# The order of the first layer's work: a rank for every piece in place of a repeating pattern

## The chip, the cores and the metric

The kernel runs on one core of a Trainium2 chip. The metric is the device time of one execution in microseconds (us); lower is better. The engines are PE (TensorE: matrix products; its loads of the fixed operand are shown apart as PEld), ACT (ScalarE), DVE (VectorE), POOL (GpSimd) and SP (SyncE, which here only starts DMAs). Each runs its own list of instructions in order, and they wait for each other on semaphores.

## The reference, cut to what matters

The whole computation has four layers of two branches each. The change touches the first layer alone. Its input is x of 2 x 1024 rows of 128. One branch puts x through eight blocks:

```python
def _block(x, p):                       # eight times, L0_attn
    residual = x
    q = x @ Wq + bq; k = x @ Wk + bk; v = x @ Wv + bv
    Q = elu(q) + 1.0; K = elu(k) + 1.0
    KV = einsum('nsh,nsh->nh', K, v);  Ksum = K.sum(axis=1)
    Z = 1.0 / (Q * Ksum[:, None, :] + EPS_Z)
    V = Q * KV[:, None, :] * Z
    attn = gelu(V @ Wo + bo)
    x = layernorm(attn + residual, ln1_s, ln1_b)
    residual = x
    h = gelu(x @ Wf1 + bf1)             # 512 wide
    ff = gelu(h @ Wf2 + bf2)
    return layernorm(ff + residual, ln2_s, ln2_b)
```

The other is a softmax attention of 16 heads of 8 columns over the same x:

```python
scores = einsum('bhqd,bhkd->bhqk', q, k) / sqrt(8)
attn = softmax(scores, axis=-1)
o = einsum('bhqk,bhkd->bhqd', attn, v)
```

What follows (output projection, a mixture of experts, three further layers) is the same in both kernels.

## The kernel before

`layer_0_branches` does both branches at once. The data are laid with the 128 features on the partitions.

**The eight blocks.** The 2048 rows are cut into four streams `s` of 512 columns. Each stream goes through eight blocks `i`. One block of one stream has 16 products of 128x128 by 128x512 in float32 on PE: `k`, `q`, `v`, `o`, `n1centre`, `n1var`, `f0` to `f3`, `ff` (four in one), `n2centre`, `n2var`. All are issued by the helper `product` (L110). A float32 product shows as two MATMUL records, two passes. Between them ACT does `exp_k`, `relu_k`, `exp_q`, `relu_q` (L586, L588), `log_z`, `z` (L592, L596), the gelus `gelu_o`, `h0` to `h3`, `gelu_ff` (L566) and the logarithm and exponential of the norms (L573, L577). DVE does the sums, products and norm scaling: `Q` and `K` at L671, `mix` at L688, `res1` and `res2` at L692 and L696, `n1copy` and `n2copy` at L653. POOL squares (L734), and at the end adds each stream to x (L738).

**The attention.** It is cut into 16 chunks `m`. A chunk has 16 units of `search` (L498: a pair of bf16 products into a PSUM buffer of 128x1024, whose maximum DVE takes in `maximum`, L708), one `turn` of the maxima (L507), 16 units of `weigh` (L523: the same scores less their maximum, into such a buffer, whose exponential ACT takes in `weight`, L622), 8 pieces of `use` (L540: the weights times the values, four 128x32 float32 products side by side on the array's columns), then `out` (L629), `sums` (L551), `log` (L638), `inverse` (L642) and on POOL a division (L744). SP carries the maxima into `qs` (L427), loads the next block's weights and later sets of `qs` and `ks`.

**The buffers.** `search` and `weigh` share two double PSUM buffers in the order in which PE comes to them: a unit can be issued when the unit two before it has been read, by DVE for a `search` and by ACT for a `weigh` (`double_free`). All other outputs but that of `use` share three single banks in the same way (`single_free`). So the order on PE also says which buffer a unit waits for. ACT needs one table for gelu and another for exp and log, and a table load stands wherever its order goes from one to the other (`logs` and `gelu`).

**What sets the order.** Each engine's work is written as several generators (the four streams, `search`, `weigh`, `use` and so on). A generator yields a planned number and then issues its instructions; `in_order` always lets the generator with the lowest number go on. The numbers are only compared, nothing waits for a time. Before, they come from a pattern of length `PERIOD = 44.0`: block `i` of stream `s` stands at `(2 * i + s // 2) * PERIOD` plus an entry of `PLAN_ATT` or `PLAN_NET`, chunk `m` at `m * PERIOD` plus an entry of `PLAN_CHUNK`. So the order of one period repeats, called a round below, and each round holds two blocks of streams and parts of three chunks.

Of the kernel before, what the change touches and what calls it, by code (L numbers as in the profile page):

```python
# [227 lines left out]
class Ring:  # L228
# [25 lines left out]
BUFS = 3  # L254

PERIOD = 44.0
PLAN_ATT = {
    "q": (3.88, 0.80), "k": (-0.00, -3.02), "v": (5.37, 1.59), "exp_k": (0.98, -1.86), "relu_k": (1.52, -0.11),
    "exp_q": (6.24, 2.05), "relu_q": (6.77, 4.58), "less_k": (3.19, -1.17), "K": (4.35, 0.58), "less_q": (13.24, 11.61),
# [4 lines left out]
PLAN_NET = {  # L264
# [5 lines left out]
PLAN_CHUNK = {  # L270
    "search": (10.34, 14.80, 15.01, 18.78, 18.99, 22.65, 22.86, 29.45, 31.73, 36.64, 37.86, 39.71, 42.80, 48.77, 51.26, 54.14),
    "maximum": (12.12, 15.22, 17.08, 19.20, 20.26, 23.42, 24.48, 29.86, 32.17, 37.06, 38.27, 40.77, 43.22, 49.19, 51.67, 54.55),
    "negate": (55.92,), "turn": (59.40,), "turn_copy": (60.83,),
# [8 lines left out]
def layer_0_branches(core, w_att, w_f1, w_f2, wa, col, att_landed, cols_landed, q_dram, k_dram, qs, ks, stacks, values, later, mixed):  # L282
# [29 lines left out]
    def att(s, i, name):  # L312
        return (2 * i + s // 2) * PERIOD + PLAN_ATT[name][s % 2]

    def net(s, i, name):
        return (2 * i + s // 2 + 1) * PERIOD + PLAN_NET[name][s % 2]

    def chunk(m, name, i=0):
        return m * PERIOD + PLAN_CHUNK[name][i]

# [3400 lines left out]
```

## Time and profile before

| what | value |
|---|---|
| median of three runs | 1711.33 us |
| the three runs | 1709.41, 1711.33, 1718.65 us |
| the profiled execution | 1713.21 us, its span 1711.5 us |
| PE busy over the span | 1571.5 us (92%) |
| first layer's branches in the trace | about 30.4 to 822 us |
| mean granted TensorE clock | 0.964 of full |

The profile was taken of one more execution, whose own time is 1713.21 us; 1.7 us of it lie outside of the span from the first to the last instruction. The rows are from that execution. In a timeline a row is one group of like instructions that follow each other: its start, its length to the end of the last, the engine and line, what is written and read, how many, and in brackets the idle time of the engine before it with what ended it. The ends of matmuls are modelled, so the distance from one start to the next is the surer reading.

### The profile page before, as it was taken

Reading aid. Unit: us, or ns where it says so; the run is one execution under the profiler, and the core shown is the slowest. Engines: PE = TensorE matmul, PEld = TensorE weight load, DVE = VectorE, ACT = ScalarE, POOL = GpSimd, SP = SyncE. Lnnn points to the kernel's source line nnn. Section 1 sums busy time; section 2 is a strip of 40 time slices with the busy share of each in tenths; the row PEclk is TensorE's granted clock in tenths of the full one; section 3 lists DMA queues with packets and bytes.
Section 4 is the critical chain, followed back from the end, with each engine's and each line's share of the span. In section 5 each row is a group of like instructions: output and inputs, shape, how many; then the busy total and the mean of one; then the engine's idle time right before and its main releaser. Section 6 shows DMA issues by size and latency. Waiting matters only on the chain. (4 is left out here: it accounts for less than half of the span.)

```text
span 1711.5 us, 19967 instructions
## 1 busy us (share of the span) xinstructions
PE 1571.5 (92%) x7054; PEld 682.4 (40%) x7054; DVE 1224.6 (72%) x1736; ACT 1151.8 (67%) x1604; POOL 262.1 (15%) x227
## 2 busy tenths in 40 slices
PE   6999999999999999999799989999877678678998
PEld 3333233333333333332344446665432455333674
DVE  5977777777777777773143325876399889997997
ACT  5688888888888888888333357534475568333663
POOL 1000111111010111111000010000179200582000
PEclk8999999999999999999999988999999889888999
DMA  6200101010010100000252112111353677630000
GB/s 199 57 12 7 25 13 26 13 25 13 7 25 7 25 13 7 13 0 1 60 101 62 37 39 64 46 39 44 99 191 130 204 232 249 177 132 12 1 1 25
DMA packets 66716, 104.18 MB, mean 61 GB/s; under 512 B 9015, under 2 KB 32534, under 8 KB 66596
## 3 DMA queue, kind: packets, MB, share of 16 engines
q1 hardware_dynamic: 55354, 65.15, 14.0%
q10 hardware_dynamic: 9216, 33.56, 6.0%
q0 software_dynamic: 2048, 4.20, 0.8%
q8 instruction: 57, 0.93, 0.2%
q14 instruction: 41, 0.34, 0.1%
HBM read 86.92 MB, written 15.87 MB: 60 GB/s over the span
## 5 line engine op out<-in xcount | busy, mean ns | idle before, releaser
L708 DVE TENSOR_REDUCE best<-quad 128x2 f32<-128x1024 f32 x256 | 309.7, 1221 | 130.5 <-PE quad L498 128.1
L622 ACT ACTIVATE weights<-quad 128x1024 f32<-128x1024 f32 x256 | 255.8, 1029 | 28.6 <-PE quad L523 28.2
L2629 PE MATMUL quad<-l_st,ident 128*128 128x512 f32 x256 | 130.3, 653 | 44.3 <-DVE l_st L2940 44.2
L540 PE MATMUL quad<-weights,values 128*32 128x512 f32 x1024 | 136.4, 605 | 0.4 <-ACT weights L622 0.4
L110 PE MATMUL quad<-q,wf 128*128 128x512 f32 x256 | 121.5, 606 | 0.7 <-DVE q L659 0.3
L110 PE MATMUL quad<-hid,wf 128*128 128x512 f32 x256 | 116.6, 599 | 0.0
L566 ACT ACTIVATE hid<-quad,col 128x512 f32<-128x512 f32 x128 | 84.9, 689 | 21.4 <-PE quad L110 21.2
L734 POOL TENSOR_TENSOR sq_all<-cen_all 128x512 f32<-128x512 f32 x64 | 65.2, 1039 | 213.9 <-DVE cen_all L653 213.9
L110 PE MATMUL quad<-sq_all,mean_w 128*128 128x512 f32 x176 | 94.7, 638 | 1.8 <-ACT sq_all L1367 0.9
L498 PE MATMUL quad<-ks,qs 48*128 48x512 bf16 x512 | 89.5, 385 | 6.8 <-DVE best L708 6.3
L2629 PEld LDWEIGHTS quad<-l_st,ident 128*128 128x128 f32 x256 | 50.7, 209 | 112.3 <-DVE l_st L2940 60.3
L523 PE MATMUL quad<-qs,ks 49*128 49x512 bf16 x512 | 91.5, 384 | 2.2 <-ACT weights L622 2.2
L744 POOL TENSOR_TENSOR mixed<-mixed,inv 128x512 f32<-128x512 f32 x16 | 20.3, 1269 | 465.9 <-ACT inv L642 465.9
L2528 POOL DMA_INDIRECT slots<-l_rows,l_blocks_index x32 | 82.0, 2562 | 42.0 <-ACT l_rows L2746 32.5
L110 PE MATMUL quad<-cur,wa 128*128 128x512 f32 x168 | 87.0, 627 | 0.0
L2923 DVE TENSOR_TENSOR l_st<-l_u,l_bs 128x1024 f32<-128x1024 f32 x64 | 76.5, 1221 | 10.7 <-PE quad L2629 10.7
L523 PEld LDWEIGHTS quad<-qs,ks 49*128 49x128 bf16 x512 | 22.2, 93 | 146.8 <-issue 60.4
L1391 ACT ACTIVATE end_hid<-quad,end_w1s 128x512 f32<-128x512 f32 x64 | 42.9, 688 | 53.5 <-PE quad L110 51.7
L2940 DVE TENSOR_TENSOR l_st<-l_st,l_c_rows 128x1024 f32<-128x1024 f32 x64 | 75.5, 1213 | 0.1
L2931 DVE TENSOR_TENSOR_SCAN l_st<-sq_all,l_st 128x1024 f32<-128x1024 f32 x32 | 71.9, 2276 | 2.2 <-ACT sq_all L2863 2.2
L110 PEld LDWEIGHTS quad<-q,wf 128*128 128x128 f32 x256 | 45.7, 189 | 66.4 <-issue 64.7
L2931 DVE TENSOR_TENSOR_SCAN l_st<-cen_all,l_st 128x1024 f32<-128x1024 f32 x32 | 71.7, 2274 | 0.0
(454 smaller groups left out, 3035.6 us busy)
## 6 DMA issues: line engine op xcount, KB each, us to landing
l_bs<-xd_dram ACTq DMA_DIRECT2D x32, 512.0 KB
l_c_rows<-xd_dram ACTq DMA_DIRECT2D x32, 512.0 KB
end_cs<-comb SPq DMA_DIRECT2D x32, 256.0 KB, 3.9
l_cs<-comb SPq DMA_DIRECT2D x32, 256.0 KB, 3.7
l_weights<-in_F_w SPq DMA_DIRECT2D x30, 257.0 KB, 4.7
wf<-in_L_f SPq DMA_DIRECT2D x16, 256.0 KB, 2.6
l_rows<-in_F_w SPq DMA_DIRECT2D x15, 257.0 KB, 6.0
qs<-q_dram SPq DMA_DIRECT2D x16, 192.0 KB, 3.5
```

The costliest lines, as they stand in the source:

```text
L110: last = nc.tensor.matmul(out[:, c:c + BANK], lhsT, rhs[:, c:c + BANK], start=(n == 0), stop=(n == len(pairs) - 1))
L498: last = nc.tensor.matmul(to[:, par * BANK:(par + 1) * BANK], qs[n % BUFS][rows, slot, qt * P:(qt + 1) * P], ks[n % BUFS][rows, slot, c * ...
L523: last = nc.tensor.matmul(to[:, par * BANK:(par + 1) * BANK], ks[n % BUFS][rows, slot, kt * P:(kt + 1) * P], qs[n % BUFS][rows, slot, c * ...
L540: last = nc.tensor.matmul(out[32 * j:32 * j + 32, :], values[:, kt, GH * g + j, :], weights[p % BUFS][:, j % 2, j // 2, :], start=(kt == 0 ...
L566: return nc.scalar.activation(*args, ACT.Gelu_apprx_tanh, **kwargs)
L622: nc.scalar.activation(weights[p % BUFS][:, slot, :, :].rearrange("p a t -> p (a t)"), doubles.of("weigh", m, i), ACT.Exp, scale=scale).th ...
L708: nc.vector.tensor_reduce(heads[:, :, slot, qt, c], doubles.of("search", m, i).rearrange("p (a t) -> p a t", a=2), AX.X, ALU.max).then_inc ...
L2528: nc.gpsimd.indirect_dma_start(slots_dram, bass.IndirectOffsetOnAxis(blocks.index[:, i, t:t + 1], 0), rows[:, t, :], None).then_inc(scatte ...
L2629: last = nc.tensor.matmul(y[d][:, c:c + BANK], core.ident[:, :], st[n % RING][:, c:c + BANK], start=False, stop=(s == NS - 1), skip_group_ ...
L2923: nc.vector.tensor_tensor(st[n % RING][:, :], u[h][d][:, :], bs[k % 2][:, :], ALU.mult).then_inc(dbx_ready, 1)
L2931: nc.vector.tensor_tensor_scan(out=st[i][:, :], data0=da[i], data1=st[i][:, :], initial=0.0, op0=ALU.mult, op1=ALU.add).then_inc(scanned, 1)
L2940: nc.vector.tensor_tensor(st[n % RING][:, :], st[n % RING][:, :], cs_rows[k % 2][:, :], ALU.mult).then_inc(times_c, 1)
```

## The change

The pattern is replaced by one table, `PLAN_0`, with a rank for each single piece of work: `PLAN_0["q"]` has 32 numbers, one for each stream and block, `PLAN_0["search"]` has 256, and so on. The ranks count up on each engine from 1 (PE to 1088, ACT to 816). The functions `att`, `net` and `chunk` now look the rank up. The DMAs of SP and the divisions and additions of POOL, whose numbers were those of another piece plus a constant, have entries of their own (`load_att`, `load_maxima`, `divide`, ...). `in_order`, the rings of buffers, the waits and all instructions stay as they are; what differs is the order on each engine, hence which buffer a unit gets, and where ACT's table loads fall.

```diff
-PERIOD = 44.0
-PLAN_ATT = {
-    "q": (3.88, 0.80), "k": (-0.00, -3.02), "v": (5.37, 1.59), "exp_k": (0.98, -1.86), "relu_k": (1.52, -0.11),
...
+PLAN_0 = {
+    "q": (5, 95, 231, 367, 500, 639, 772, 907, 3, 90, 229, 358, 496, 628, 770, 905, 14, 159, 294, 436, 572, 703, 838, 979, 28, 158, 295, 427, 561,
+        698, 833, 975,),
...
+    "load_att": (3, 8, 14, 21, 26, 32, 38,),
...
+    def at(name, i):
+        return PLAN_0[name][i]
+
     def att(s, i, name):
-        return (2 * i + s // 2) * PERIOD + PLAN_ATT[name][s % 2]
-
-    def net(s, i, name):
-        return (2 * i + s // 2 + 1) * PERIOD + PLAN_NET[name][s % 2]
+        return at(name, s * B + i)
+
+    net = att
 
     def chunk(m, name, i=0):
-        return m * PERIOD + PLAN_CHUNK[name][i]
+        return at(name, m * (len(PLAN_0[name]) // CHUNKS) + i)
...
-                        yield att(fourth, i - 1, "o") + 1
+                        yield at("load_att", i - 1)
...
-                        yield chunk(m, "inverse") + 1
+                        yield at("divide", m)
```

The line numbers of what follows the table move by 131: L110 stays, L498 becomes L629, L523 becomes L654, L540 becomes L671, L708 becomes L839, L622 becomes L753.

The order on PE at the start of the layer, before. Rows with `xn,wa` are `k`, `q` and `v`, `mq,wa` is `o`, `k,centre_w` a centring, `sq_all,mean_w` a variance, `ks,qs` a `search` (two matmuls a unit):

```order
L110 MATMUL quad<-xn,wa 128x512 x6
L498 MATMUL quad<-ks,qs 128x512 x14
L110 MATMUL quad<-mq,wa 128x512 x2
L110 MATMUL quad<-k,centre_w 128x512
L498 MATMUL quad<-ks,qs 128x512 x2
L110 MATMUL quad<-k,centre_w 128x512
L498 MATMUL quad<-ks,qs 128x512 x2
L110 MATMUL quad<-sq_all,mean_w 128x512
```

The same place with the change:

```order
L110 MATMUL quad<-xn,wa 128x512 x6
L629 MATMUL quad<-ks,qs 128x512 x6
L110 MATMUL quad<-mq,wa 128x512
L629 MATMUL quad<-ks,qs 128x512 x2
L110 MATMUL quad<-mq,wa 128x512
L110 MATMUL quad<-xn,wa 128x512 x2
L629 MATMUL quad<-ks,qs 128x512 x4
L110 MATMUL quad<-k,centre_w 128x512 x2
```

Seven searches stood ahead of the first `o`; now three do, and `k` and `q` of the third stream follow the two `o`.

The order on PE in the middle of the layer, before, the same in each round. `qs,ks` is a `weigh` (two matmuls a unit), `weights,values` a `use` (four):

```order
L523 MATMUL quad<-qs,ks 128x512 x2
L498 MATMUL quad<-ks,qs 128x512 x2
L540 MATMUL quad<-weights,values 32x512 x4
L523 MATMUL quad<-qs,ks 128x512 x2
L540 MATMUL quad<-weights,values 32x512 x4
L523 MATMUL quad<-qs,ks 128x512 x4
L110 MATMUL quad<-sq_all,mean_w 128x512 x2
L523 MATMUL quad<-qs,ks 128x512 x2
L498 MATMUL quad<-ks,qs 128x512 x2
L540 MATMUL quad<-weights,values 32x512 x4
```

The same work with the change, in the fifth round:

```order
L654 MATMUL quad<-qs,ks 128x512 x2
L629 MATMUL quad<-ks,qs 128x512 x2
L110 MATMUL quad<-sq_all,mean_w 128x512
L654 MATMUL quad<-qs,ks 128x512 x4
L671 MATMUL quad<-weights,values 32x512 x8
L654 MATMUL quad<-qs,ks 128x512 x4
L110 MATMUL quad<-sq_all,mean_w 128x512 x2
L629 MATMUL quad<-ks,qs 128x512 x4
L671 MATMUL quad<-weights,values 32x512 x8
```

Two pieces of `use` now mostly stand together (x8), and after a `search` there often comes a single product and then the next pair of score units, where a `use` stood between.

The order on ACT at the end of the layer, before. `hid` are the `h0` to `h3`, `mk` the two `gelu_ff`, `weights` the `weight` units of the last chunk:

```order
L566 ACT_TABLE_LOAD
L566 ACTIVATE hid<-quad,col 128x512 x8
L561 ACT_TABLE_LOAD
L642 ACTIVATE inv<-inv 128x512
L566 ACT_TABLE_LOAD
L566 ACTIVATE mk<-quad,col 128x512 x2
L561 ACT_TABLE_LOAD
L622 ACTIVATE weights<-quad 128x1024 x3
L629 ACTIVATE mixed<-quad 128x512
```

With the change:

```order
L697 ACT_TABLE_LOAD
L697 ACTIVATE hid<-quad,col 128x512 x8
L692 ACT_TABLE_LOAD
L773 ACTIVATE inv<-inv 128x512
L753 ACTIVATE weights<-quad 128x1024 x2
L697 ACT_TABLE_LOAD
L697 ACTIVATE mk<-quad,col 128x512 x2
L692 ACT_TABLE_LOAD
L753 ACTIVATE weights<-quad 128x1024
L760 ACTIVATE mixed<-quad 128x512
```

Two of the last chunk's sixteen `weight` units are moved ahead of the two `gelu_ff`.

## Rows read from the trace of the kernel before

**Rows 1.** The page, busy time, share of the span and instructions of PE.

```profile
PE 1571.5 (92%) x7054; PEld 682.4 (40%) x7054; DVE 1224.6 (72%) x1736; ACT 1151.8 (67%) x1604; POOL 262.1 (15%) x227
```

**Rows 2.** Three stretches: length, busy time by engine (count), clock, DMA share, GB/s.

```profile
30.40:85.00 54.60, 47.15 (x121) 15.93 (x121) 46.13 (x71) 35.26 (x48) 3.48 (x5) 0.87 0.40 112
85.00:776.00 691.00, 690.07 (x2823) 213.88 (x2822) 513.48 (x746) 606.39 (x791) 81.30 (x79) 1.00 0.06 14
776.00:822.00 46.00, 39.35 (x183) 11.54 (x179) 11.12 (x17) 37.24 (x46) 8.57 (x8) 1.00 0.00 1
```

**Rows 3.** The waits of PE from 129 to 786 us: total, times, longest.

```profile
PE quad L523 <- ACT weights L622: 0.4, 1, 0.4
```

**Rows 4.** The timeline of PE in the middle of the layer.

```profile
476.47 0.39 PE L523 MATMUL quad<-qs,ks 49*128 49x512 bf16 x2
476.79 1.07 PE L540 MATMUL quad<-weights,values 128*32 128x512 f32 x8
477.79 0.61 PE L523 MATMUL quad<-qs,ks 49*128 49x512 bf16 x4
478.32 1.98 PE L110 MATMUL quad<-sq_all,mean_w 128*128 128x512 f32 x4
...
480.47 0.38 PE L498 MATMUL quad<-ks,qs 48*128 48x512 bf16 x2
...
482.17 0.39 PE L523 MATMUL quad<-qs,ks 49*128 49x512 bf16 x2
482.49 1.12 PE L110 MATMUL quad<-sq_all,mean_w 128*128 128x512 f32 x2
483.55 0.39 PE L523 MATMUL quad<-qs,ks 49*128 49x512 bf16 x2
...
500.39 4.56 PE L110 MATMUL quad<-q,wf 128*128 128x512 f32 x10
504.88 0.60 PE L498 MATMUL quad<-ks,qs 48*128 48x512 bf16 x4
```

**Rows 5.** The page, costliest groups: busy, mean ns of one, idle before.

```profile
L708 DVE TENSOR_REDUCE best<-quad 128x2 f32<-128x1024 f32 x256 | 309.7, 1221 | 130.5 <-PE quad L498 128.1
...
L110 PEld LDWEIGHTS quad<-q,wf 128*128 128x128 f32 x256 | 45.7, 189 | 66.4 <-issue 64.7
```

**Rows 6.** The timeline of PE at the start of the layer.

```profile
43.74 0.61 PE L498 MATMUL quad<-ks,qs 48*128 48x512 bf16 x2 [1.12 <-DVE best L708]
45.47 0.61 PE L498 MATMUL quad<-ks,qs 48*128 48x512 bf16 x2 [1.12 <-DVE best L708]
...
47.25 3.78 PE L110 MATMUL quad<-mq,wa 128*128 128x512 f32 x4
```

**Rows 7.** The timeline of DVE at the start of the layer.

```profile
43.59 0.68 DVE L671 SCALAR_TENSOR_TENSOR q<-q,mq 128x512 f32<-128x512 f32 x1
44.19 2.35 DVE L708 TENSOR_REDUCE best<-quad 128x2 f32<-128x1024 f32 x2
46.46 1.40 DVE L688 SCALAR_TENSOR_TENSOR mq<-q,totals,mk 128x512 f32<-128x512 f32 x2
```

**Rows 8.** A stretch at the start: length, PE busy (count), clock, DMA share, GB/s.

```profile
46.00:50.00 4.00, 3.43 (x8) 0.50 0.54 115
```

**Rows 9.** The timeline of ACT at the end of the layer.

```profile
795.33 0.69 ACT L566 ACTIVATE mk<-quad,col 128x512 f32<-128x512 f32 x1 [2.48 <-PE quad L110]
796.03 1.28 ACT L561 ACT_TABLE_LOAD   x1
797.33 2.86 ACT L622 ACTIVATE weights<-quad 128x1024 f32<-128x1024 f32 x3
...
816.69 0.60 ACT L629 ACTIVATE mixed<-quad 128x512 f32<-128x512 f32 x1 [0.68 <-PE quad L540]
```

**Rows 10.** The timeline of POOL at the end of the layer.

```profile
810.86 1.27 POOL L738 TENSOR_TENSOR x<-x,cur 128x512 f32<-128x512 f32 x1 [4.61 <-DVE cur L659]
...
819.84 1.26 POOL L744 TENSOR_TENSOR mixed<-mixed,inv 128x512 f32<-128x512 f32 x1 [2.48 <-ACT inv L642]
```

More of the change, by code:

```diff
@@ L392, in block_weights @@
                         sp.dma_start(wa[:, :], w_att[i]).then_inc(att_landed, 16)
-                        yield net(fourth, i - 1, "f3") + 1
+                        yield at("load_f1", i - 1)
                         sp.wait_ge(st.pe_done[third], spe.value("f3", i - 1))
@@ L396, in block_weights @@
                         sp.dma_start(wf1[:, :], w_f1[i]).then_inc(f1_landed, 16)
-                        yield net(fourth, i - 1, "ff") + 4
+                        yield at("load_f2", i - 1)
                         sp.wait_ge(st.pe_done[third], spe.value("ff", i - 1))
@@ L415, in sets @@
                     for n in range(BUFS, len(SETS)):
-                        yield chunk(2 * (n - BUFS) + 1, "use", PAIRS - 1) + 2
+                        yield at("load_set", n - BUFS)
                         sp.wait_ge(weights_used, 2 * PAIRS * (n - BUFS + 1))
@@ L422, in maxima_rows @@
                         n, c = m // 2, m % 2
-                        yield chunk(m, "turn_copy") + 0.5
+                        yield at("load_maxima", m)
                         sp.wait_ge(turned_copied, m + 1)
@@ L734, in stream @@
                             nc.gpsimd.tensor_tensor(st.sq[s], st.cen[s], st.cen[s], ALU.mult).then_inc(st.pool_done[s], 1)
-                    yield net(s, B - 1, "n2affine") + 1
+                    yield at("add", s)
                     pool.wait_ge(st.dve_done[s], sdve.value("n2affine", B - 1))
@@ L747, in second_values @@
                     for g in range(GROUPS):
-                        yield chunk(2 * g + 1, "use", PAIRS - 1) + 3
+                        yield at("second", g)
                         pool.wait_ge(weights_used, 2 * PAIRS * (g + 1))
```

118 lines of the change are left out of this document (108 added, 10 removed), and 48 rows, old and new, of tables (PLAN_0, PLAN_ATT, PLAN_NET).

## The prediction, made before the changed kernel ran

> **What bounds the kernel now.** I read first the busy shares: PE 92% [rows 1]. That is an average over four layers, and the change touches one, so next come the three stretches of that layer [rows 2]. From 85 to 776 us PE is busy 690.07 of 691.00 us at full clock, ACT 606 and DVE 513: PE is the bound, with no other engine near. Ahead of it lie 54.60 us with 47.15 of PE work at a clock of 0.87, behind it 46.00 us with 39.35. Last the waits: from 129 to 786 us PE waited once, 0.4 us [rows 3]. So in the middle an order can gain only by making PE's own work cheaper, and can lose by any wait that it brings; gains by better filling are to be had at the two ends alone, where PE idles 7.5 and 6.7 us.
>
> **PE's own work.** The same matmuls run, but what one costs depends on its neighbours, start to start [rows 4]. A run of five products takes 504.88 - 500.39 = 4.49 us, two 478.32 to 480.24 or 1.92 us, one alone among score units 483.55 - 482.49 = 1.06: about 0.86 each and 0.10 at either end of a run. A `weigh` ahead of a `use` takes 476.79 - 476.47 = 0.32, two units ahead of products 478.32 - 477.79 = 0.53, so a further unit is 0.22. A lone `use` takes 477.79 - 476.79 = 1.00. I laid these distances on the order of all 1088 pieces. Before that gives 765 us. With the change the products and score units come to the same within 0.5 us (products 0.7 less, searches 1.5 less, weighs 1.7 more): runs are cut and joined about equally often. The `use` pieces change: before, one pair among 128 stood together, now 48 follow another `use`. The trace has no such pair that was not held up by a wait, so I bound it. Below: the second costs as a product within a run, 0.86, and the first leaves off its end too, which saves about 0.2 a pair or 10 us. Above: nothing is saved, and some pieces gain a costlier neighbour, +0.6. I take the value of a switch of kind saved once, 0.10: each such pair costs 0.91 + 1.00 in place of about 2.0. 48 x 0.10 = 4.8, with the 0.5 of the rest **-5.1 us**, ends -10 and +0.6.
>
> What decides this is whether the fixed operand of the next `use` is loaded while the last one still streams. A 128x128 load takes 189 ns [rows 5], and in a run a pass starts each 0.45 us (ten in 4.49 [rows 4]), hardly longer than its 512 columns need; so loads are hidden behind passes that use the same rows of the array. The Trainium skill, page "TensorE: Matmul & The Clock Gate", section "The mechanism", says that a weight load overlaps running matmuls "only when row_grp differs"; two `use` pieces both use all rows, so by it the pair saves nothing. The row speaks against that rule, and with the rule this term would be +0.6 rather than -5.1.
>
> **Waits that the new order brings.** A `search` gives its buffer back after DVE's reduction. At the start, where DVE is the limit and PE idles before each, the searches stand 45.47 - 43.74 = 1.73 us apart [rows 6]; that is PE's 0.43, the 1.22 us reduction [rows 5] and the signals. In the old middle the shortest way from a `search` to the unit that takes its buffer is 482.17 - 480.47 = 1.70 [rows 4], a `use` between; no wait is seen there. The new order has 41 places where a `search`, one product and two score units, or the like, leave only 0.31 + 1.06 + 0.22 = 1.59. Each must wait 0.13 to 0.14: 41 x 0.13 = **+5.3 us**. Where the reduction is itself queued behind another DVE operation (0.60 us from 43.59 to 44.19 [rows 7]) or a `weight` behind another on ACT (0.92 each, 2.86 for three [rows 9]), I find about a dozen places short by 0.1 to 0.6, the worst in the fourteenth round where a copy precedes the maximum: **+3.5**. What waits is PE, and all else is behind it.
>
> Chains over two engines are also tighter. After `o` the matching centring needs PE's 1.1, a gelu of 0.69 [rows 9], an addition of 0.68 like that in [rows 7] and signals, 2.7 us; the old order left 1.6 us more than that, the new one in three of 32 places nothing. In four rounds the logarithm of the mixing is put between `h1` and `h3`, with two more table loads in three of them (66 table changes become 72), so `ff` waits for `h3` behind it. Each load is 1.3 us of ACT (796.03 to 797.33 [rows 9]); six are 8 us, and ACT has 691 - 606 = 85 us idle in the middle [rows 2], so they count only where `ff` follows at once. I set these chains at **+2.5**, between 0 and 8 (half a microsecond in each of 16 rounds). The Trainium skill, page "ScalarE: Activation LUTs", section "What ACT_TABLE_LOAD costs", puts a change of table at about 2.66 us with a drain of 1380 ns; here the next activation starts 1.30 us after the load, so the trace does not show that drain. By the page the six would be 16 us of ACT, still under its idle time.
>
> SP's order also moves. What counts there is the maxima: their four DMAs must land before the chunk's first `weigh`. By the same prices the new order leaves 5.7 us or more from `turn` to `weigh` where the old one left 11; no load is queued ahead that waits longer. I put this at 0.
>
> **The start.** Before, seven searches stand ahead of the first `o` on PE, and the reductions keep DVE from `mix`, which runs at 46.46 [rows 7]; the two `o` start at 47.25 [rows 6], and at a clock of 0.50 [rows 8] take 3.8 us. With the change both `Q` come first on DVE, then one reduction, then `mix` of the first stream. Five reductions stood ahead of it, now one; at (46.46 - 44.19) / 2 = 1.13 each `mix` moves to 46.46 - 4 x 1.13 = 41.9, so the first `o` can start near 42.9, the second near 45, and `k` and `q` of the third stream fill PE's time that was idle. Fewer searches are done by then (six in place of seven at 49.5). Going on along both engines by the same distances I come to the first `turn` about 3 us earlier; the reductions that bound this part are as many. I take **-3.5 us**, between -1 and -5. The clock also rises earlier if PE is busy earlier; that is inside this range.
>
> **The end.** ACT idles 2.48 us ahead of the last `gelu_ff` [rows 9]. Two `weight` units now go there, 2 x 0.92 = 1.8 us off a tail in which ACT then works through to 816.69 - 0.68 = 816.0. Against it the last exponential of a norm is put behind `out` (816.69 before), so that POOL's last addition, which ended at 812 [rows 10], ends some 0.6 us later than the last division could have begun. **-1.2 us**, between -2 and +0.5.
>
> **The sum:** -5.1 + 5.3 + 3.5 + 2.5 - 3.5 - 1.2 = +1.5 us. Against the profiled execution, 1713.21, that is 1714.7; its time stands 1.9 above the median of the three runs, so for a median I predict **1713 us**, no change that can be told. About 0.5% (8.6 us) is what a measurement of this kernel can tell from none: faster is below 1702.8, slower above 1719.9.
>
> **Rivals.** (1) *PE's work gets clearly cheaper and the waits are smaller.* Pairs of `use` save their full 0.2 (-10), the short places mostly lie behind time lost elsewhere (+2 in place of 5.3 + 3.5), and the chains hold (+2.5): -10 + 2 + 2.5 - 4.5 - 1.5 = -11.5, 1700 us. For it: the long run of products shows joined pieces at their cheapest. Against it: the distances 1.59 and 1.73 are both read off directly. (2) *DVE's queue, slower.* In each of the 41 short places the reduction must find DVE free. If in four of ten a 0.60 us operation [rows 7] stands ahead of it, a place costs 0.13 + 0.24 = 0.37 and the term is 15 in place of 5.3: +1.5 + 10 = +11.5, 1723 us. It ends on the slower side from a mean of 0.3 a place on. For it: DVE is 513 of 691 us busy in the middle. Against it: I counted most of such cases already and found few; the old order kept 1.70 at least everywhere. (3) *Pairs of `use` save nothing,* which is what the rule on weight loads above would give: -5.1 becomes +0.6, the sum +7.2, 1718.5, still no change that can be told. (4) *The new ranks do not change the order that matters*, that is, all terms are under 1 us: 1711. The order as built speaks against it.
>
> **How the numbers follow.** Forecast 0.42 and rival 4 0.03, both within 0.5%; rival 3 0.13, of which I give 0.04 to a little over the bound; rival 1 0.22; rival 2 0.20. So faster 0.22, same 0.54, slower 0.24. The range runs from 1700 (rival 1) to 1723 (rival 2); cases beyond, all waits and no saving or the reverse, are left with about 2 in 10. The forecast alone, with the ends of its terms, is 1704 to 1720.
>
> **What would show it.** In the changed profile: (a) the pairs of `use` as rows with x16 whose distance to the next row is 1.91 (right) or 2.0 (rival 3) or 1.8 (rival 1); (b) waits of PE in the middle on DVE's reduction, some 40, total 5 us, where there were none; a total over 12 is rival 2; (c) PE's row for the first `o` at about 43 us; (d) the first `turn` about 3 us earlier; (e) ACT without the 2.5 us gap ahead of the last `gelu_ff`, and the layer's last division within 2 us of 819.84 in place of clearly ahead of it. The forecast is wrong if the middle stretch is over 8 us longer or shorter than before, or if anything after the layer differs by more than 2 us.

## The result: seven to nine microseconds slower, and where they are

| | before | changed |
|---|---|---|
| median of ten runs | 1716.91 us (1709.41 to 1721.36) | 1723.76 us (1716.57 to 1729.09) |
| ratio, 95% interval | | 1.005 (1.003 to 1.007) |
| profiled execution, its span | 1713.21 us, 1711.5 us | 1725.14 us, 1723.4 us |
| first product of the layer to its last `sums` | 786.86 us | 794.68 us |

The kernel is slower, by 0.3 to 0.7%, at the border of what can be told. The predicted 1713 us missed by 10.8 us. 5.6 us of that is the base: the three runs given had a median of 1711.33, ten runs of the same kernel 1716.91. The rest is the layer, forecast at +1.5 us and measured at +7.8 in the profiles. Of the twelve executions of the second kernel with new ranks further down, one fell in a slower state (2576.11 us at a granted clock of 0.554) and is left out of its median.

The page of the changed kernel, and three stretches of it with the windows of [rows 2]:

```profile
PE 1582.0 (92%) x7054; PEld 691.1 (40%) x7054; DVE 1237.4 (72%) x1736; ACT 1157.7 (67%) x1610; POOL 268.9 (16%) x227
```

```profile
30.40:85.00 54.60, 48.72 (x124) 16.15 (x123) 47.12 (x72) 35.35 (x49) 2.76 (x5) 0.85 0.43 112
85.00:776.00 691.00, 680.67 (x2769) 217.02 (x2768) 516.28 (x735) 604.11 (x784) 83.34 (x76) 1.00 0.06 14
776.00:822.00 46.00, 45.49 (x219) 13.60 (x217) 18.66 (x25) 41.98 (x52) 8.15 (x7) 1.00 0.01 1
```

In the middle PE is now busy 680.67 of 691 us where it was 690.07, and has issued 2769 passes where it had issued 2823. It is behind; besides, three products (six passes) that stood in the middle before now stand outside of it. These are the landmarks on PE (the first product, the first `weigh`, the last `turn`, the last `sums`), first before, then changed:

```profile
30.48 1.19 PE L110 MATMUL quad<-xn,wa 128*128 128x512 f32 x1 [5.61 <-PEq L811]
...
85.07 0.60 PE L523 MATMUL quad<-qs,ks 49*128 49x512 bf16 x4
...
788.01 0.27 PE L507 MATMUL quad<-ident,neg 128*16 128x128 f32 x1
...
817.34 1.13 PE L551 MATMUL quad<-mixed,spread 128*128 128x512 f32 x2 [0.72 <-ACT mixed L629]
```

```profile
29.72 2.04 PE L110 MATMUL quad<-xn,wa 128*128 128x512 f32 x2 [5.67 <-PEq L942]
...
83.64 0.39 PE L654 MATMUL quad<-qs,ks 49*128 49x512 bf16 x2
...
793.79 0.27 PE L638 MATMUL quad<-ident,neg 128*16 128x128 f32 x1
...
824.40 1.12 PE L682 MATMUL quad<-mixed,spread 128*128 128x512 f32 x2 [0.72 <-ACT mixed L760]
```

Start: 54.59 us before, 53.92 now. Middle, from first `weigh` to last `turn`: 702.94, now 710.15. End: 29.33, now 30.61. What follows the layer takes 894.2 us of one span and 899.0 of the other; over all profiles of this study, whose programs differ in this layer alone, it lies between 891 and 904.3, so that difference says nothing, and the prediction's bound of 2 us on it could not tell anything. Inside the layer like distances repeat to some 10 ns; the changed kernel's middle and that of the run on the start further down, which differs from it in the first chunk alone, are 710.15 and 710.27 us. No kernel was profiled twice, but by this I read differences of tenths of a microsecond there from one profile.

**Work and wait, parted.** The view of PE's waits does not show what happened: from 85 to 793 us it adds up to 9 us, because a wait that is shorter than the modelled end of the matmul ahead of it isn't seen as idle time. The distances from start to start show all of it. I took the price of each kind of piece between each pair of neighbours from the places where neither it nor the next was released within the last 0.2 us, summed these prices over the order (own work), and called the rest of each distance wait, put down to the release it follows:

| middle (us) | length | own work | wait | after a reduction | after an exponential | chains and others |
|---|---|---|---|---|---|---|
| before | 702.94 | 695.1 | 7.8 | 2.2 (16) | 4.8 (60) | 0.4 |
| changed | 710.15 | 683.5 | 26.7 | 11.3 (56) | 6.3 (44) | 8.2 |

(In brackets the number of places; rests under 0.02 us a place are in the wait alone.) Own work is 11.6 us less, waits are 18.9 us more. Not all of the 11.6 is saved: the change puts four more products behind the last `turn` and one less ahead of the first `weigh`, so the middle has three fewer, at 0.86 us each some 2.6 us. Over the whole layer own work falls by 9.5, from 760.4 to 750.9.

A joined pair of `use`, and four of the places after a reduction, both on PE of the changed kernel:

```profile
399.34 1.93 PE L671 MATMUL quad<-weights,values 128*32 128x512 f32 x16
401.20 0.39 PE L654 MATMUL quad<-qs,ks 49*128 49x512 bf16 x2
...
778.45 0.39 PE L629 MATMUL quad<-ks,qs 48*128 48x512 bf16 x2
778.77 1.07 PE L671 MATMUL quad<-weights,values 128*32 128x512 f32 x8
779.77 0.39 PE L654 MATMUL quad<-qs,ks 49*128 49x512 bf16 x2
780.18 0.39 PE L629 MATMUL quad<-ks,qs 48*128 48x512 bf16 x2
...
781.56 0.39 PE L654 MATMUL quad<-qs,ks 49*128 49x512 bf16 x2
781.90 0.39 PE L629 MATMUL quad<-ks,qs 48*128 48x512 bf16 x2
...
783.28 0.39 PE L654 MATMUL quad<-qs,ks 49*128 49x512 bf16 x2
783.61 0.39 PE L629 MATMUL quad<-ks,qs 48*128 48x512 bf16 x2
```

The pair takes 1.86 us, not 2.00. The searches at 778.45, 780.18, 781.90 and 783.61 stand 1.73, 1.72 and 1.71 apart; one `weigh` lies between, so each takes the buffer of the last. From `weigh` to `search` it is 0.41, 0.34 and 0.33 where 0.23 would do. No row has an idle time in brackets, yet PE loses about 0.1 to 0.2 at each. DVE shows the same rhythm from the other side, a reduction each 1.71 us with 0.49 of idle time, waiting for the search that waits for it:

```profile
780.62 1.23 DVE L839 TENSOR_REDUCE best<-quad 128x2 f32<-128x1024 f32 x1 [0.49 <-PE quad L629]
782.33 1.23 DVE L839 TENSOR_REDUCE best<-quad 128x2 f32<-128x1024 f32 x1 [0.49 <-PE quad L629]
784.04 1.23 DVE L839 TENSOR_REDUCE best<-quad 128x2 f32<-128x1024 f32 x1 [0.49 <-PE quad L629]
```

**Something not foreseen: DVE and POOL hold each other up.** Five of PE's six longest waits in the middle (1.47, 1.40, 1.05, 0.77 and 0.74 us) follow DVE operations that took two to four times their time. DVE, POOL and PE of the changed kernel:

```profile
401.71 1.50 DVE L799 TENSOR_SCALAR mq<-mq 128x512 f32<-128x512 f32 x1
403.14 2.34 DVE L839 TENSOR_REDUCE best<-quad 128x2 f32<-128x1024 f32 x2
...
405.69 0.42 DVE L799 TENSOR_SCALAR mq<-mq 128x512 f32<-128x512 f32 x1
```

```profile
401.64 1.30 POOL L875 TENSOR_TENSOR mixed<-mixed,inv 128x512 f32<-128x512 f32 x1 [16.32 <-ACT inv L773]
```

```profile
402.80 0.39 PE L629 MATMUL quad<-ks,qs 48*128 48x512 bf16 x2
404.50 0.39 PE L629 MATMUL quad<-ks,qs 48*128 48x512 bf16 x2 [1.31 <-DVE best L839]
```

L799 takes 0.42 us alone and 1.50 when it begins beside the division: it ends 0.27 us after the division does (403.21 against 402.94). Of the layer's DVE operations that read and write SBUF alone (L787, L790, L799, L819, L823), 15 began while POOL was at work; 12 were stretched, and the other three came in its last 0.25 us. Of 42 that read PSUM (reductions, copies) none was. The other way round, 16 of 18 POOL operations that began beside a DVE operation on SBUF alone took longer than usual, a square up to 1.49 us in place of 1.04. The kernel before had 13 such meetings, always `mix` (L688, 1.07 in place of 0.74) under the division, with slack behind it. This agrees with the Trainium skill, page "SBUF — State Buffer", section "SBUF: two separate sides", by which the two engines share a pair of ports under an exclusive lock.

### The profile page after: what moved, and what is told of

Same layout as the page of the kernel before. It is cut to its first block and busy times, and to the rows that moved or that the text cites. A ratio compares the mean times of both kernels' runs of the same rounds, so it can differ in the third digit from the quotient of the medians.

```text
span 1723.4 us, 19973 instructions
## 1 busy us (share of the span) xinstructions
PE 1582.0 (92%) x7054; PEld 691.1 (40%) x7054; DVE 1237.4 (72%) x1736; ACT 1157.7 (67%) x1610; POOL 268.9 (16%) x227
## 5 line engine op out<-in xcount | busy, mean ns | idle before, releaser
L839 DVE TENSOR_REDUCE best<-quad 128x2 f32<-128x1024 f32 x256 | 308.9, 1222 | 105.8 <-PE quad L629 104.4
L753 ACT ACTIVATE weights<-quad 128x1024 f32<-128x1024 f32 x256 | 255.0, 1028 | 33.0 <-PE quad L654 30.1
L865 POOL TENSOR_TENSOR sq_all<-cen_all 128x512 f32<-128x512 f32 x64 | 70.4, 1117 | 517.1 <-DVE cen_all L784 517.1
L671 PE MATMUL quad<-weights,values 128*32 128x512 f32 x1024 | 127.1, 600 | 0.1
L110 PE MATMUL quad<-q,wf 128*128 128x512 f32 x256 | 123.0, 613 | 0.1
L110 PE MATMUL quad<-hid,wf 128*128 128x512 f32 x256 | 117.5, 601 | 0.9 <-issue 0.5
L629 PE MATMUL quad<-ks,qs 48*128 48x512 bf16 x512 | 90.6, 387 | 9.6 <-DVE best L839 8.5
L110 PE MATMUL quad<-sq_all,mean_w 128*128 128x512 f32 x176 | 95.2, 639 | 1.8 <-ACT sq_all L1498 0.9
L654 PE MATMUL quad<-qs,ks 49*128 49x512 bf16 x512 | 91.3, 384 | 2.4 <-ACT weights L753 0.9
L110 PE MATMUL quad<-cur,wa 128*128 128x512 f32 x168 | 84.4, 617 | 1.7 <-issue 1.5
L654 PEld LDWEIGHTS quad<-qs,ks 49*128 49x128 bf16 x512 | 21.7, 93 | 130.8 <-ACT weights L753 68.2
L110 PEld LDWEIGHTS quad<-hid,wf 128*128 128x128 f32 x256 | 46.3, 190 | 57.7 <-issue 57.7
L110 PEld LDWEIGHTS quad<-q,wf 128*128 128x128 f32 x256 | 44.4, 190 | 57.4 <-issue 42.7
```

Of the source, the lines that this page charges most:

```text
L110: last = nc.tensor.matmul(out[:, c:c + BANK], lhsT, rhs[:, c:c + BANK], start=(n == 0), stop=(n == len(pairs) - 1))
L629: last = nc.tensor.matmul(to[:, par * BANK:(par + 1) * BANK], qs[n % BUFS][rows, slot, qt * P:(qt + 1) * P], ks[n % BUFS][rows, slot, c * ...
L654: last = nc.tensor.matmul(to[:, par * BANK:(par + 1) * BANK], ks[n % BUFS][rows, slot, kt * P:(kt + 1) * P], qs[n % BUFS][rows, slot, c * ...
L671: last = nc.tensor.matmul(out[32 * j:32 * j + 32, :], values[:, kt, GH * g + j, :], weights[p % BUFS][:, j % 2, j // 2, :], start=(kt == 0 ...
L753: nc.scalar.activation(weights[p % BUFS][:, slot, :, :].rearrange("p a t -> p (a t)"), doubles.of("weigh", m, i), ACT.Exp, scale=scale).th ...
L839: nc.vector.tensor_reduce(heads[:, :, slot, qt, c], doubles.of("search", m, i).rearrange("p (a t) -> p a t", a=2), AX.X, ALU.max).then_inc ...
```

## The experiments

All but two are read from one profile each. "Wait" is counted as above.

**POOL's work cut (three runs).** The squares are cut from the second block on, in the first run those of `n1`, in the second those of `n2`; both cut the divisions too, and the third run cuts the divisions alone (the `.then_inc(...)` behind each call is left out here):

```diff
-nc.gpsimd.tensor_tensor(st.sq[s], st.cen[s], st.cen[s], ALU.mult)
+w = 64 if pre == "n1" and i > 0 else TS
+nc.gpsimd.tensor_tensor(st.sq[s][:, 0:w], st.cen[s][:, 0:w], st.cen[s][:, 0:w], ALU.mult)
-nc.gpsimd.tensor_tensor(heads_of(m), heads_of(m), inv[:, :], ALU.mult)
+nc.gpsimd.tensor_tensor(heads_of(m)[:, 0:64], heads_of(m)[:, 0:64], inv[:, 0:64], ALU.mult)
```

> The changed kernel with POOL's work cut: from the second block on the squares of the first norm, and all sixteen divisions, are done for 64 of their 512 columns (the rest is left out); the squares of the second norm and the order of everything stay. In the changed kernel the way from the first weigh (83.64 us) to the last turn (793.79 us) is 710.15 us, against 702.94 before. Theory C: POOL's long operations stretch DVE operations that run beside them (L799 at 401.71 took 1.50 us beside a division, L787 at 682.10 took 1.53 beside a square, each about twice its usual time), and PE's longest waits are behind those. Then here the stretched operations under divisions and first squares are gone (401.71, 444.39, 529.5, 682.10), PE's waits of 1.47 us at 402.8, 0.74 at 444.4 and 1.05 at 682.9 are down to under 0.3, and the way is 4 to 8 us shorter. Theory R: the waits come from the reduction's and exponential's turnaround in the tighter order alone. Then the way is shorter by under 2 us, and those three waits are still there.

Measured: middle 706.75 us, 3.4 shorter. The wait at 444.4 is gone, that at 682.9 is 0.30 in place of 1.05, that at 402.8 is 0.52 in place of 1.47, where under 0.3 was expected.

> As the run with the first norm's squares cut, but here the squares of the second norm (from the second block on) and all divisions are cut to 64 of 512 columns, the rest left out, and the first norm's are whole. Theory C: the two stretches of 1.55 us of L823 at 280.0 and 671.56, which begin under second or first squares that stand in a row of two or three, are gone or smaller in one of the two runs; each wait of PE behind them (0.77 at 280.5, 1.40 at 672.7) goes with it. The way from the first weigh to the last turn is 4 to 8 us shorter than 710.15. Theory R: under 2 us shorter.

Measured: 706.65, 3.5 shorter; the wait of 0.77 at 280.5 is gone, that of 1.40 is 0.61.

> The changed kernel with POOL's sixteen divisions alone cut to 64 of 512 columns (the rest is left out); all squares are whole. With the two runs that cut divisions and one kind of square (middles of 706.75 and 706.65 us against 710.15) this parts POOL's share. The stretched DVE operations under divisions are those at 401.71 (1.50 us) and 444.39 (1.60 us), behind which PE waited 1.47 and 0.74; so the middle should be 2 to 3 us shorter than 710.15, 707 to 708, and the whole of POOL's share is then the sum of the two runs less this one, 4 to 5 us. If the squares matter alone it is within 0.5 us of 710.15.

Measured: 708.18, 2.0 shorter. The same places with the small division, on DVE and POOL:

```profile
401.39 0.55 DVE L799 TENSOR_SCALAR mq<-mq 128x512 f32<-128x512 f32 x1
401.87 2.34 DVE L839 TENSOR_REDUCE best<-quad 128x2 f32<-128x1024 f32 x2
```

```profile
401.31 0.35 POOL L875 TENSOR_TENSOR mixed<-mixed,inv 128x64 f32<-128x64 f32 x1 [16.32 <-ACT inv L773]
```

L799 is back at 0.55. A shorter square also ends its own chain earlier, which could have been the gain instead. But PE's order is the same in these runs, so the distances can be compared piece by piece: in each run nearly all that is gained is gained at three to six places (of 404.50, 446.09, 684.91, 281.61, 674.30, 532.02 and 484.61), all behind stretched operations. If the parts add up, POOL's whole share is (710.15 - 706.75) + (710.15 - 706.65) - (710.15 - 708.18) = 4.9 us of the 18.9. Theory C holds in kind; the first two runs came in under its 4 to 8, and it explains a quarter of the new waits, not most.

**Half of each reduction.** In both kernels:

```diff
-doubles.of("search", m, i).rearrange("p (a t) -> p a t", a=2),
+doubles.of("search", m, i).rearrange("p (a t) -> p a t", a=2)[:, :, 0:256],
```

> The changed kernel, each maximum over 256 of each 512 columns (the other half is left out), so that a reduction takes about 0.65 us in place of 1.22 and DVE is some 145 us less busy. All else is as it was. Every theory in which PE waits for DVE (the turnaround of 1.70 us from a search to the unit that takes its buffer, DVE's queue, and the stretched operations) says that the middle loses most of its 24.6 us of waits, by my count down to under 9, and is 12 to 18 us shorter than 710.15. If the waits were ACT's (table loads, the exponential's turnaround of 1.53), it would be shorter by under 5.

Measured: 700.12, 10.0 shorter, a little under the range. Waits after a reduction fall from 11.3 to 0.9; those after an exponential stay (7.6), and so do the chains (6.4).

> The kernel before, each maximum over 256 of each 512 columns (the other half is left out). Its middle, from the first weigh at 85.07 to the last turn at 788.01, has 5.7 us of waits by my count and was PE-bound; so it stays within 4 us of 702.94, and only the start, where DVE is the limit, is shorter. This is the ground for the term of PE's own work: with the waits on DVE gone from both, the changed kernel's middle should be shorter than this one's by that term. The prediction had 5.1 us; by the distances in the changed kernel's trace (a pair of use in 1.86 us in place of 2.0) I count 11.7. If it is under 3, joined pieces of use save nothing.

Measured: 702.82, as expected. But the changed kernel without these waits is only 2.7 us shorter. That is under the 3 us at which I was to conclude that joined pieces save nothing. The conclusion does not hold, since 16.6 us of other waits were left in the changed kernel, far more than my first count; so this pair could not give own work; the pair with all cover off, below, asks again.

**DVE's and POOL's order alone.** Only the order on these two engines differs, as in

```diff
-    "divide": (14, 18, 23, 32, 34, 40, 45, 54, 58, 65, 66, 71, 76, 83, 87, 89,),
+    "divide": (14, 17, 24, 27, 32, 42, 47, 52, 53, 61, 68, 74, 77, 83, 86, 88,),
```

> The changed kernel with only the ranks of DVE and POOL changed from 80 us on (510 of 768 pieces on DVE, most by one to three places); PE and ACT keep the changed kernel's order word for word, so PE's own work must be the same. The ranks were looked for with the durations and distances of the traces so far, such that a maximum finds DVE free and few DVE operations begin beside one of POOL's. Theory Q (the waits come from what stands ahead on DVE's queue, POOL's stretching counted in): the middle, 710.15 us in the changed kernel, becomes 700 to 703, that is 7 to 10 us shorter; no wait of over 1 us is left. Theory T (PE's own tight order makes the waits, a search with less than 1.70 us to the unit that takes its buffer): DVE's order can't help, the middle stays within 2 us of 710.

Measured: 702.65, 7.5 shorter, with PE's order untouched: theory Q. Chains lost 4.2 us of wait, reductions 2.5. Two fifths of what the middle lost to waits can be had back by when DVE and POOL do things; the 8.8 us that stay after reductions lie at PE's own short distances.

**PE's order alone, from the kernel before.** The old pattern was written as ranks, then those of PE changed.

> The kernel before with only PE's ranks changed from 80 us on (423 of 1088 pieces, most by one to three places); ACT, DVE and POOL keep the old order. 24 pieces of use follow another use where one did, and 200 runs of products stand where 209 did. By the distances in the traces of both kernels (use after use 0.86 to 0.88 us for the first, 0.97 for the last, 1.00 alone) PE's own work in the middle falls from 697.2 us by 4.2, and its waits stay at 5 to 6. Expected middle 697 to 699 in place of 702.94. If a pair of use saves nothing, by the other distances the fall is under 1 us and the middle is 702 to 703.

Measured: 701.34, 1.6 shorter, outside of the range. By the common prices own work is 690.2, 4.9 less with 22 pairs in the middle; but waits rose from 7.8 to 11.1, about 1.5 us of it behind reductions and 2.2 in products and pieces of `use` that came late by other ways. It is the whole case in small: by the count the joined pieces save what they should, and the tighter order gives two thirds of it back.

**Tables.** Both kernels, every gelu of the layer replaced:

```diff
-table[0] = "gelu"
-return nc.scalar.activation(*args, ACT.Gelu_apprx_tanh, **kwargs)
+logs()
+return nc.scalar.activation(*args, ACT.Relu, **kwargs)
```

> The changed kernel with Relu in place of every gelu of the layer, so that ACT needs no second table and its 72 table loads of 1.28 us are gone (the result is another one). PE's own work is the same. By the distances of the traces the chains over ACT (h3 to ff, mix to o, the exponential behind a table load) lose about 4 us of waits in the middle: 706 in place of 710.15. If table loads cause most of the new waits the middle falls below 702; if none, it stays at 709 to 710.

Measured: 705.42, 4.7 shorter.

> The kernel before with Relu in place of every gelu of the layer (the result is another one), so its 66 table loads are gone. Its chains had slack, so the middle should stay at 702.0 to 702.9 in place of 702.94. What the run of the changed kernel without tables gains over this one is what the new order pays for tables.

Measured: 700.76, 2.2 shorter, more than expected: the kernel before paid for tables too. The new order pays 2.5 us more. An activation takes as long with either function (0.69 us), so the loads are what differs.

**The start.** Each search of the first chunk but the first is issued three times:

```diff
+for again in range(3 if m == 0 and i else 1):
     last = nc.tensor.matmul(to[:, par * BANK:(par + 1) * BANK], qs[n % BUFS][rows, slot, qt * P:(qt + 1) * P],
...
```

> The changed kernel with each search of the first chunk but the first one issued three times into the same buffer, with the same result: 0.46 us more work of PE for each, in the time in which PE waits for DVE's reductions (0.9 us ahead of each). It keeps PE busy while DVE is the limit. Theory K (the gain forecast for the start was lost to the clock: 0.50 at 42 to 46 us and 0.81 or less after 54 us, behind idle stretches of PE): the granted clock no longer falls after 50 us and falls less at 42 to 50, and the first turn comes 1 to 3 us earlier than 42.9 us behind the first product. Theory D (DVE is the limit whatever PE's clock is): the first turn stays within 0.5 us of 42.9.

Measured: the clock no longer falls after 54 us, but the first `turn` comes 44.6 us after the first product, 1.7 later. The stretch from 58 to 62 us (length, PE, PEld, DVE, ACT, POOL busy, clock, DMA share, GB/s), in the changed kernel and in this one:

```profile
58.00:62.00 4.00, 4.00 (x9) 0.74 (x8) 2.92 (x5) 2.03 (x4) 0.00 (x0) 0.50 0.00 0
```

```profile
58.00:62.00 4.00, 4.00 (x16) 1.23 (x16) 3.50 (x4) 2.52 (x4) 0.96 (x1) 1.00 0.00 0
```

Neither theory's number came out. The edit also delays each reduction by the extra passes, so it can't part the two; what the clock costs the start is left open.

**All cover off.** Reductions and exponentials halved, no tables, PE untouched, in both kernels. Beside the two edits above:

```diff
+w = 2 * BANK if p < BUFS else BANK
-nc.scalar.activation(weights[p % BUFS][:, slot, :, :].rearrange("p a t -> p (a t)"), doubles.of("weigh", m, i),
+nc.scalar.activation(weights[p % BUFS][:, slot, :, :].rearrange("p a t -> p (a t)")[:, 0:w], doubles.of("weigh", m, i)[:, 0:w],
```

> The changed kernel with light work on the other engines: maxima over 256 of each 512 columns, exponentials of the weights over 512 of 1024 columns after the first three pairs (the rest is left out, stale values stay), Relu for gelu so that no table is loaded. PE's instructions and their order are untouched. If PE's own work is 683.5 us in the middle, as I count it from distances without a wait, and few waits are left, the middle is 684 to 688 in place of 710.15. If own work is really about 690 (5 us less than before), it is over 690.

> The kernel before with the same light work: half maxima, half exponentials, no table loads; PE untouched. By the distances its own work in the middle is 695.1 us, so the middle is 695 to 697 in place of 702.94. The changed kernel's should then be 8 to 11.6 us shorter than this; 5 or less would say that the forecast's 5.1 was right.

First `weigh` and last `turn` on PE, of the changed kernel so lightened and of the one before:

```profile
80.43 0.60 PE L654 MATMUL quad<-qs,ks 49*128 49x512 bf16 x4
...
768.84 0.27 PE L638 MATMUL quad<-ident,neg 128*16 128x128 f32 x1
```

```profile
80.86 0.60 PE L523 MATMUL quad<-qs,ks 49*128 49x512 bf16 x4
...
776.41 0.27 PE L507 MATMUL quad<-ident,neg 128*16 128x128 f32 x1
```

688.41 and 695.55 us. The second is the own work counted for before (695.1) within 0.5. The first is 7.1 us shorter, where 8 to 11.6 was expected, with 4.9 us of waits still found in it, which gives 683.5 again. The three products that the middle of the changed kernel lacks are in the 7.1. From the first `turn` to the last `sums`, where the changed kernel does the same work and two searches more, the lightened kernels take 728.80 and 733.94 us. So 5.1 us of cheaper work are shown by the two spans alone, as much as was forecast; what lies above that, up to some 9.5 over the layer, rests on the count of the waits that are left.

**A version that keeps the saving.** If cheaper work was real and the waits a matter of order, ranks chosen for both should beat both kernels. They were looked for piece by piece with the distances and durations of these traces. The table itself tells a reader nothing; at the place of [rows 4] PE of the second such kernel runs:

```profile
479.32 0.39 PE L546 MATMUL quad<-ks,qs 48*128 48x512 bf16 x2
479.54 0.38 PE L571 MATMUL quad<-qs,ks 49*128 49x512 bf16 x2
479.85 1.92 PE L588 MATMUL quad<-weights,values 128*32 128x512 f32 x16
481.71 0.39 PE L546 MATMUL quad<-ks,qs 48*128 48x512 bf16 x2
481.94 0.38 PE L571 MATMUL quad<-qs,ks 49*128 49x512 bf16 x2
```

A joined pair stands between units that share a buffer, so they are 2.4 us apart and no wait arises.

> The changed kernel with new ranks on PE, ACT, DVE and POOL from 65 us on, looked for with the distances and durations of the traces so far: pairs of use stay joined (40 of them), but a buffer is not asked for before its reader can be done, and DVE operations keep clear of POOL's. If the explanation holds (joined pieces save about 10 us of PE's own work in the middle, and the new waits, not anything in the rest of the program, gave them back), the middle is 689 to 693 us in place of 710.15 and 702.94, and the whole is 9 to 13 us shorter than the kernel before, a ratio of 0.993 to 0.995. If the layer's length is given back in the later layers, the ratio is 1.00.

Measured: middle 698.18 us (own work 685.2, waits 13.0). Whole: median 1708.07 us of six runs, ratio to the kernel before 0.9952 (0.9923 to 0.9981).

> The same made from the order of the kernel before: its start is kept up to 62 us, the ranks after that are new on PE, ACT, DVE and POOL (32 pairs of use joined, 66 changes of ACT's table as before). The middle is 690 to 694 us in place of 702.94, the end about 2 us shorter, the whole 10 to 14 us shorter than the kernel before, a ratio of 0.992 to 0.995. If the gain of joined pairs were not real, the middle could be no shorter than 700.

Measured: middle 697.03 (own work 686.2, waits 10.8). Whole: median 1708.72 us of eleven runs, ratio 0.9949 (0.9930 to 0.9969); the kernel before had 1715.82 over nineteen runs beside them. Both middles are 3 to 5 us over their ranges, since more waits are left (11 to 13 us) than I had counted on. The ratios lie at the near end of what was expected, the medians are 7.8 and 7.1 us shorter where at least 9 and 10 were. The layer itself is 6.5 and 7.8 us shorter in the profiles, so the gain is not given back in the later layers.

## Why the prediction was wrong

The layer was to take 1.5 us more and took 7.8 more, 6.3 over the forecast. By the count above this is made up of waits in the middle (+7.6), waits at the start (+3.6), waits at the end (-0.4) and own work over the layer (-4.4). Two steps failed toward the slow side. The start: the saving of 3.5 us did not come, as waits there are what they were. The chains: put at 2.5 us, they and the other places without a shared score buffer cost 7.8, and what stretches DVE's operations stood in no term at all. The terms one by one:

- **PE's own work (-5.1).** Right in kind, too small: -9.5 over the layer, near rival 1's -10. A pair of `use` costs 1.86 us, the distance that rival 1 had named as its sign (1.8) rather than the forecast's (1.91), so a pair saves 0.14, 6.7 us for 48. What was mis-sized is "the value of a switch of kind saved once"; this error alone would have made the kernel faster than forecast. The remaining 2.8 us are units and products with cheaper neighbours, which I had at 0.5 (and 4.8 with 0.5 is 5.3, not 5.1).
- **Rival 3** is refuted by the same row and by the lightened pair. The rule of the Trainium skill that I had weighed (page "TensorE: Matmul & The Clock Gate", section "The mechanism") does not describe these `use` pieces.
- **The 41 short places (+5.3).** Mechanism, number and price were right. The places after a reduction rose from 16 to 56; some 46 of the 56 cost under 0.2 us each, 0.12 on average. What was too small is the tail: ten longer ones cost 5.8 us together, 1.47, 1.40 and 0.76 the longest, the first two behind DVE operations that POOL had stretched. In all they cost 9.1 us more than before. And a sentence of the step was false: it took the 1.70 us of 480.47 to 482.17 [rows 4] as a distance at which "no wait is seen". It was itself such a wait, of 0.14, in each round of the kernel before (2.2 us); the view of waits cannot show it.
- **Other short places (+3.5).** Partly inside the above; those after an exponential cost 1.5 more. Together the two terms were 8.8 us, and 10.6 were measured. Places without a release near cost 1.4.
- **Chains (+2.5).** +6.4, within the 0 to 8 given. Two causes were sized wrongly: tables, which were to count only where `ff` follows at once, cost 2.5 us over all; and DVE's stretched operations, 4.9 us over all kinds, were in no term. All the waits together were put at 11.3 us and were 18.9.
- **The middle** came out near its forecast (+7.2 against +6.2) by luck: two errors, -6.5 on work (2.6 of it products done elsewhere) and +7.6 on waits, nearly cancelled.
- **The start (-3.5).** The first `o` does come at 41.59 (11.9 us after the first product in place of 16.8), as said, but the first `turn` only 0.5 us earlier in this count, and its waits don't change: 14.9 and 15.0 us beyond own work at full clock. This is the step "going on along both engines by the same distances I come to the first `turn` about 3 us earlier". From the first product to that `turn`, first before, then changed:

```profile
30.48:73.94 43.46, 36.09 (x90) 11.73 (x90) 35.51 (x59) 26.97 (x38) 3.44 (x5) 0.84 0.50 140
```

```profile
29.72:72.64 42.92, 37.20 (x86) 12.17 (x87) 34.90 (x53) 26.60 (x37) 3.44 (x5) 0.81 0.53 142
```

  DVE has 35.51 and 34.90 us of work in it. Of the other 8 us, 3.5 lie ahead of its first operation, so no order of DVE could have given 3 us unless nearly all its idle time went. I had followed `mix` forward and not asked what DVE still owes before the `turn`. PE also ran at 0.81 of its clock there in place of 0.84, with a second fall to 0.50 at 58 to 62 us; with the halved reductions the `turn` is only 2.5 us earlier, so DVE is not the only limit either.
- **The end (-1.2).** About right: waits fell by 1.6. The stretch is 1.3 us longer all the same, as four more products stand in it. ACT's rows, with the line from the last hidden gelu at 797.61:

```profile
797.61 0.69 ACT L697 ACTIVATE hid<-quad,col 128x512 f32<-128x512 f32 x1 [0.17 <-PE quad L110]
798.32 1.28 ACT L692 ACT_TABLE_LOAD   x1
799.61 0.63 ACT L773 ACTIVATE inv<-inv 128x512 f32<-128x512 f32 x1
801.43 1.94 ACT L753 ACTIVATE weights<-quad 128x1024 f32<-128x1024 f32 x2 [1.19 <-PE quad L654]
803.39 1.28 ACT L697 ACT_TABLE_LOAD   x1
804.68 1.27 ACT L697 ACTIVATE mk<-quad,col 128x512 f32<-128x512 f32 x2
...
823.75 0.60 ACT L760 ACTIVATE mixed<-quad 128x512 f32<-128x512 f32 x1
```

  The gap of 2.48 us [rows 9] is gone and one of 1.19 is left. From the last hidden gelu to the last `out` it takes 26.1 us where it took 28.5. The layer's last division does not begin within 2 us of its old 819.84 [rows 10] all the same, but at 827.49, since all ahead of it is late: 3.09 us behind the start of the last `sums`, 0.59 more than before, which is the delay that the prediction named.
- **Rival 2** named the right time (1723) for a part of the reason: a mean of 0.2 a place, not 0.37, and the rest from chains, tables and POOL. That it met the time is luck besides, since 5.6 us of it are the base.
- **The base.** The forecast stood on a median of three runs that the next seven moved by 5.6 us, two thirds of the bound for a change. A range around it has to hold that as well. The range of the terms was too narrow too: their own ends, added up, give -8.2 to +16.9, or 1703 to 1728, where the prediction wrote 1704 to 1720.

## What to carry to other kernels

Where PE is full, count its work by distances from start to start, and get the price of a piece from places with slack on both sides: a view of idle time misses all waits of 0.1 to 0.2 us, and here they were 18 of 27 us. Joining like pieces is worth real time (0.14 us a pair here), but only where the units that share a buffer end up as far apart as their reader needs; put the joined pair between them. And before an operation of POOL is moved, look at which DVE operations it will meet.

## What the runs showed of the hardware

- Two `use` pieces in a row (eight 128x32 float32 products) take 1.86 us, 0.88 and 0.97, against 1.00 alone; three take 0.86 for the one between.
- The way from a search to the unit that takes its buffer is nowhere in the middle of the two kernels under 1.70 us: 0.42 to the reduction's start, 1.22 in it, 0.06 back.
- A DVE operation from SBUF to SBUF that begins beside a POOL operation ends 0.3 to 0.5 us after it (0.42 became 1.50, 0.68 became 1.55), and a POOL square that begins beside such a DVE operation takes up to 1.49 us in place of 1.04. Operations of DVE that read PSUM were not touched, 42 of 42.
- Behind a product that had to wait, the next product in the run comes 0.10 us later than its price (the wait of 0.68 at 177.52, the 0.10 at 178.48); the count above puts this under waits.
